# Issuing the stacked query and key loads of layer 2 earlier, and starting the layer's projection work later

## The reference, cut to what matters

```
qkv = x @ qkv_w + qkv_b ; reshape(n, t, 3, H, DH)
attn = einsum('nthd,ntkd->nthk', q * scale, k) ; softmax over k
out = einsum('nthk,ntkd->nthd', attn, v) ; out.transpose(0, 2, 1, 3).reshape(n, t, d)
x = x + gate_msa * (out @ proj_w + proj_b)
x = x + gate_mlp * (gelu(modulate(layernorm(x)) @ fc1_w + fc1_b) @ fc2_w + fc2_b)
```

## Time and profile before

| | |
|---|---|
| median of three runs | 2290.39 us (2288.09 to 2295.49) |
| the profiled execution's own time | 2290.39 us |
| its span | 2288.5 us |
| mean granted TensorE clock | 0.937 of full speed |
| TensorE matmul busy | 2037.6 us, 89% of the span |
| VectorE, ScalarE, GpSimd busy | 57%, 51%, 21% |
| DMA: moved over the span | 173.97 MB, mean 76 GB/s |
| attention and feed-forward of loops 8 to 11 | from 1450 to 1850 us |

### The profile page before, as it was taken

How to read it: one execution, slowest core, us unless ns; L and a number is a source line. 1 busy time by engine, 2 the same in 40 slices (tenths; PEclk the granted TensorE clock), 3 DMA queues, 4 the chain that set the end, 5 groups by cost and what they waited for, 6 DMA issues and landing times.

```text
span 2288.5 us, 39073 instructions
## 1 busy us (share of the span) xinstructions
PE 2037.6 (89%) x15592; PEld 1508.4 (66%) x15592; DVE 1302.8 (57%) x2781; ACT 1162.7 (51%) x1801; POOL 482.1 (21%) x502
## 2 busy tenths in 40 slices
PE   6978898899989998999889899989997898999988
PEld 4347387568856885688465556888786546474748
DVE  4757546646574757475747482453444758474733
ACT  2444724654555545555635555553444474647363
POOL 3022114414420433143210100032120102000001
PEclk9788999899999998999899999999898899999999
DMA  5343323342233223323331412356154131314111
GB/s 158 80 125 57 104 78 88 62 139 63 80 82 95 72 84 62 110 80 81 86 88 14 129 7 63 50 102 122 32 98 115 20 111 33 89 22 105 17 14 24
DMA packets 204731, 173.97 MB, mean 76 GB/s; under 512 B 54822, under 2 KB 164678, under 8 KB 204550
## 3 DMA queue, kind: packets, MB, share of 16 engines
q1 hardware_dynamic: 197974, 158.76, 29.9%
q0 software_dynamic: 6576, 12.71, 2.0%
HBM read 125.57 MB, written 40.11 MB: 72 GB/s over the span
## 4 chain that ended last, share of the span: by engine, by line
PE 56%; DVE 21%; ACT 13%; issue 3%; POOL 3%; DMA 2%; SPq 2%; ACTq 0%; POOLq 0%; DVEq 0%
PE PSA L1853 13%; PE PSA L1868 11%; DVE MX L1506 8%; PE PSA L1757 5%; PE PSA L1647 5%; ACT PB L1342 4%; PE PSA L1734 4%; PE PSA L1704 4%; PE PSA L1747 4%; POOL FL L1240 2%; DVE HH L1626 2%; PE PSA L1716 2%; DVE FH L1391 2%; PE PSA L1777 1%; ACT HH L1379 1%
## 5 line engine op out<-in xcount | busy, mean ns | idle before, releaser
L1506 DVE TENSOR_REDUCE MX<-PSA 128x1 f32<-128x512 f32 x768 | 489.7, 683 | 307.5 <-PE PSA L1734 304.6
L1853 PE MATMUL PSA<-A,FH 128*128 128x256 f32 x2520 | 440.7, 289 | 25.6 <-DVE HH L1626 20.3
L1868 PE MATMUL PSA<-FH,HH 128*128 128x288 f32 x2016 | 451.2, 315 | 10.5 <-DVE HH L1626 10.5
L1379 ACT ACTIVATE HH<-PSA 128x512 fp32r<-128x512 f32 x252 | 150.4, 597 | 591.6 <-PE PSA L1853 584.3
L1342 ACT ACTIVATE PB<-PSA 128x1024 f32<-128x1024 f32 x384 | 370.8, 1028 | 103.5 <-PE PSA L1747 103.0
L1853 PEld LDWEIGHTS PSA<-A,FH 128*128 128x128 f32 x2520 | 359.6, 192 | 49.6 <-issue 26.4
L1868 PEld LDWEIGHTS PSA<-FH,HH 128*128 128x128 f32 x2016 | 332.7, 197 | 51.6 <-issue 38.2
L1868 PE MATMUL PSA<-FL,HH 128*128 128x288 f32 x1008 | 304.7, 302 | 0.0
L1245 POOL TENSOR_TENSOR X<-X,TM 128x288 f32<-128x288 f32 x176 | 139.0, 804 | 721.3 <-DVE TM L1571 721.2
L1240 POOL TENSOR_TENSOR FL<-ST,FH 128x544 fp32r<-128x544 f32 x171 | 238.8, 1410 | 235.0 <-ACT FH L1372 235.0
L1734 PE MATMUL PSA<-KS,QS 54*128 54x512 f32 x768 | 225.3, 512 | 43.4 <-DVE MX L1506 20.8
(11 more groups left out here) (163 smaller groups left out, 2378.0 us busy)
## 6 DMA issues: line engine op xcount, KB each, us to landing
qkd<-HH SPq DMA_DIRECT2D x48, 504.0 KB
ST<-in_L_cond_w SPq DMA_DIRECT2D x51, 432.0 KB
ST<-in_L_cond_w SPq DMA_DIRECT2D x102, 192.0 KB
QS<-qkd SPq DMA_DIRECT2D x88, 144.0 KB
KS<-qkd SPq DMA_DIRECT2D x88, 144.0 KB
QS<-qkd SPq DMA_DIRECT2D x144, 72.0 KB
KS<-qkd SPq DMA_DIRECT2D x144, 72.0 KB
ST<-in_L_cond_w SPq DMA_DIRECT2D x153, 48.0 KB
```

The costliest lines, as they stand in the source:

```text
L1379: e.activation(r(HH[u][:, 0, :]), PS[bk][:, :], gelu)
L1506: e.reduce_max(MX[p // 2 % 2][:, col:col + 1], PS[bk][:, :], axis=AX.X).then_inc(free[bk], 1)
L1853: m = e.matmul(PS[bk][:, s_ * 256:(s_ + 1) * 256], r(w_), r(x_[:, half * 256:(half + 1) * 256]), start=(z == 0), stop=(z == 6))
L1868: m = e.matmul(PS[bk][:, 0:C], r(HH[u][:, c, tk]), r(w_), start=False, stop=(j == NCH - 1 and z == 2))
```

## The change

Two start values are raised: `mid` starts at 8000 instead of 6000 planned ns in loops 8, 9 and 10, and at 14000 instead of 11000 in loop 11. `stack(i)` for units 9, 10 and 11 moves from behind the attention steps of the unit before to the end of `proj_qk2(i)`, which is reached at the sixth of the eleven attention steps. Unit 8's stack stays in `proj_v2`.

```diff
-MID_AT = (6000, 11000)
+MID_AT = (8000, 14000)
@@ proj_qk2
             qw[f] += 16 if t < 4 else 32
             hf_free[f] = (s_qw[f], qw[f])
             yield
+        if i > 8:
+            stack(i)
@@ plan, main loop
             drain(nxt)
-            if 8 < i + 1 < 12:
-                stack(i + 1)
             if i:
                 finish_bg(1000)
```

## The result

The changed kernel takes 2316.7 us (median of 4 runs, 2305.5 to 2325.5) against 2289.7 us before (2288.1 to 2295.5). Over all 21 runs of the changed kernel the ratio is 1.0103, 95% interval 1.0076 to 1.0131: it is slower by 1%. The profiled execution took 2315.4 us with a span of 2313.4.

A forecast was written before the change was run, and what follows sets the result against it. TensorE, busy for 89% of the span, was taken as the bound. Stalls 18.5, clock 3.4 and later start 2.4, less 3.7 gained in loop 11, made 20.6 us slower: 2311.0 us, range 2299 to 2324.

The forecast's parts named there:

- step 1: On SyncE, the wait for the stores of t = 4 to land ends 8.1 us after the gate load's issue.
- step 2: On SyncE, issuing the eight stack loads takes 7.7 us; then the second scr issue starts 0.6 us after the first.
- step 3: scr's landing, queued behind the stack loads, takes 7.0 us instead of 3.4 to 4.5 alone.
- step 4: From OT's issue to the end of GpSimd's copy takes 4.9 us, with 0.1 us from scr's landing to OT's issue.
- The stalls: TensorE waits for the attention output 8.9, 0.7 and 8.9 us in loops 8, 9 and 10, in sum 18.5 us.
- The clock: TensorE runs at a lower clock after the two long stalls, losing 1.7 us each, 3.4 us in all.
- The later start in loops 8 to 10: Feed-forward transposes come one step later, so TensorE's wait for normalized rows grows 0.8 us per loop, 2.4 us in all.
- Loop 11: The later start fills 3.3 us of the 5.5 us wait for the attention output; net 3.7 us gained.
- The earlier scores bring nothing: First scores fed by the moved stack come earlier, but did not wait for loads before: a reordering at no gain.
- the transfers barely meet: Rival: the stack's wait ends early and scr passes among the loads at its own 3.4 us; 2293.7 us, chance 0.15.
- all is hidden: Rival: output ready before TensorE comes for it in every loop, start values pay; 2283.7 us at best, chance 0.10.
- the late landing of loop 11: Rival: stores land as late as in loop 11, delaying stack, scr and OT 4.8 us; up to 2338.5 us, chance 0.10.

The follow-up runs named there:

- e2: Kernel before with only the later start values (8000 and 14000), the stack at its old place; 2290.7 us, ratio 0.9996.
- e4: Changed kernel, but the first scores of units 9 to 11 keep their old place; 2312.3 us, ratio 1.0095.
- e3: Kernel before, with only the first scores of units 9 to 11 at the earlier place, loads still late; 2297.9 us, ratio 1.0037.
- e1: Changed kernel with the old start values 6000 and 11000, so the stack's move alone; 2317.8 us, ratio 1.0115.
- e8: Changed kernel with only four of the eight stack loads early, the other four behind scr and OT; 2302.9 us, ratio 1.0038.
- e9: Kernel before with unit 12's twelve loads behind scr and OT and unit 10's first scores earlier; 2282.0 us, ratio 0.9956.
- e5: Changed kernel with first scores at their old place and the eight loads back behind OT, only SyncE's wait early; 2294.1 us, ratio 1.0022.

## Why the prediction was right

Direction and cause were right, and the measured time, 2316.7 us, lies in the range. Against the profiled executions the sum was 20.6 us forecast and 20.8 us measured in loops 8 to 11, but that close a match is luck, since errors cancel. In loops 8 to 10 24.3 us were forecast (18.5 of stalls, 3.4 of clock, 2.4 of the later start) and 25.2 measured: 12.9 of stalls, 7.7 of TensorE's busy time at a lower clock and 4.6 of other waits.

- *When the stack's wait ends* (step 1): 8.1 us after the gate load forecast; 8.1, 7.9 and 8.0 measured.
- *The eight issues* (step 2): 7.7 us forecast, 5.1 to 5.3 measured with what lies in between. This term was too large. The row I took it from had the OT load in front and went at 0.4 us for three loads and then at 1.1 to 1.5; behind the wait that lets the stores land, six loads are issued at 0.3 to 0.6 us each before the pace falls to 1.2 us.
- *scr's issue to OT's issue* (step 3): 0.6 + 7.0 + 0.1 = 7.7 us forecast; 7.8, 9.3 and 8.1 measured, so scr does stand behind the loads. *OT and the copy* (step 4): 4.9 forecast, 4.6 to 4.9 measured.
- *The stalls*: 8.9, 0.7 and 8.9 us forecast, 6.1, 0 and 6.8 measured. The difference is step 2's.
- *The clock*: 3.4 us forecast; TensorE's busy time grew by 4.3, 0.9 and 2.5 us in loops 8 to 10. Too small. The stretch at the lower clock is no longer than the one in loop 11, 6 to 7 us in both, but there the clock fell 2.2 us into the wait and 3.4 us of work lay in the stretch, while in loop 8 it fell some 4.5 us into the wait and 5.1 us of work lay in it. And at the end of loop 8 the changed kernel has 17 us at the lower clock where the kernel before has 10.
- *The later start in loops 8 to 10*: 0.8 us each forecast; e2 shows +3.2, -1.1 and -0.6. Near in sum (1.5 against 2.4), wrong in kind: in loop 8 it is the norm's chain behind the bias split, not the transposes' place. The waits for XN, which were to grow by 2.4 us, are 11.8 us in loops 8 to 10 after the change against 11.4 before.
- *Loop 11*: -3.7 forecast, -4.4 measured (e2: -3.6). Right.
- *The earlier scores bring nothing*: right for the change (e4). But the loads were not as free as I said: at the scores' early place in loop 8 the old loads would be 3.8 us late (e3).
- *Left out*: what stands behind GpSimd's copy. The prediction followed SyncE and TensorE and stopped at the copy; in loop 9 its delay went on into the weight loads and residual additions, a wait of 3.5 us. e1, with the same late copy (1611.7 there), had none of it, while e4 and e8 had 2.9 and 2.7 us and e2 none, so it takes the late copy and the later start together.

The rivals: that the transfers barely meet fell with step 3; that all is hidden fell with e1; the late landing of loop 11 did not come. The statement of the Trainium skill on ring order (page "DMA: Bandwidth & Descriptors", section "Queues, rings and completion order") agrees with the time from scr's issue to OT's issue: 7.8 us behind eight loads and 6.6 behind four (e8), against 4.4 with none in front. Its advice to issue a transfer early ("Rules for kernel authors") was no help here, since the consumer did not wait and the transfers behind it had one that did.

What stays open: the medians differ by 27 us, 23.9 with all 21 runs of the changed kernel (median 2315.0) against the 23 runs of the kernel before beside e1 (2291.1), and the loops by 20.8. The rest is of the size of what executions differ by ahead of loop 8 (below), and was not settled.

## What to carry to other kernels

A queue that one engine issues is a shared resource: before moving a transfer forward, list what it is moved past and who waits for that, on every engine down the line, not for the moved transfer alone. Here no consumer waited for the moved loads, and each load in front of the attention output cost once the slack was used (2 us in loop 8 at the old start, 3.8 at the new one); looking for the same pattern elsewhere (twelve loads in front of the same store in loop 11) gave a gain of 0.4%.

In this kernel a start value that trades one stall for another was worth little beside the order of the queue: three settings of it on the old order had ratios of 1, 0.9996 and 1.0011.

## What the runs showed of the hardware that was not expected

Executions of identical instruction lists differ ahead of the first changed instruction: the last maxima transpose in front of loop 8 started at 1371.1 us in the quickest profile and at 1382.9 us in the slowest of eleven. In the first 100 us the granted clock was 0.83 and 0.74 in two of them, e9 and e1; but e5, with 0.76 there, reached the same transpose at 1371.2, so where the difference comes from is open. From loop 11's end to the end of the program the eleven executions took 437.6 to 441.5 us. A comparison of single executions by the same instructions leaves these differences out and is therefore sharper here than one by their totals.
